# A shallower pipeline over slices in the projection and routing stage, and GpSimd's scatters ahead of later powers

## The reference, cut to what matters

```
x = x + 0.5 * ffn(layernorm(x))
x = x + attn(layernorm(x))
x = x + 0.5 * ffn(layernorm(x))

def ffn(x):
    x = x + msa(layernorm(x, ln1))              # 16 heads of width 8, softmax, projection w_proj
    xf = layernorm(x, ln2)
    expert = argmax(xf @ gate_w + gate_b)       # 8 experts, one per token
    return x + gelu(xf @ w1[expert]) @ w2[expert]
```

## Time and profile before

| | us |
|---|---|
| median of three runs | 1501.73 (1501.5 to 1503.06) |
| the profiled execution | 1514.03 |
| its span in the trace | 1512.0 |
| first projection stage, DVE's first instruction | 427.48 |
| first copy of the expert stage behind it | 509.48 |
| second projection stage, DVE's first instruction | 1319.35 |

### The profile page before, as it was taken

How to read it: one execution, slowest core, us unless ns; L and a number is a source line. 1 busy time by engine, 2 the same in 40 slices (tenths; PEclk the granted TensorE clock), 3 DMA queues, 4 the chain that set the end, 5 groups by cost and what they waited for, 6 DMA issues and landing times. The chain is left out here.

```text
span 1512.0 us, 39416 instructions
## 1 busy us (share of the span) xinstructions
PE 1236.6 (82%) x12592; PEld 694.6 (46%) x12593; DVE 1070.4 (71%) x1896; ACT 856.2 (57%) x1710; POOL 645.7 (43%) x741
## 2 busy tenths in 40 slices
PE   5599999999966497388888747699999999783793
PEld 3234333343356496144455434243333333383793
DVE  8689999999454232478888757899999999182232
ACT  3178888888920253443334315288888888620451
POOL 4304432343337264366665632423323433346362
PEclk9789999999985698599899859599999999865897
DMA  5513342222001121100000005221111211001224
GB/s 175 167 33 88 95 111 62 52 59 47 12 1 48 48 67 50 41 2 3 3 3 2 3 1 223 57 59 49 54 50 50 55 45 44 2 13 53 54 67 122
DMA packets 81640, 81.93 MB, mean 54 GB/s; under 512 B 16265, under 2 KB 53868, under 8 KB 81536
## 3 DMA queue, kind: packets, MB, share of 16 engines
q1 hardware_dynamic: 72704, 70.01, 16.9%
q0 software_dynamic: 4608, 8.44, 1.7%
q10 hardware_dynamic: 4224, 2.10, 0.5%
HBM read 50.56 MB, written 29.93 MB: 53 GB/s over the span
## 5 line engine op out<-in xcount | busy, mean ns | idle before, releaser
L834 DVE TENSOR_REDUCE maxima<-ps 128x2 f32<-128x1024 f32 x512 | 624.1, 1226 | 56.6 <-PE ps L661 47.3
L816 ACT ACTIVATE probs<-ps 128x512 f32<-128x512 f32 x1024 | 552.9, 598 | 78.6 <-PE ps L688 53.2
L661 PE MATMUL ps<-k_stack,q_stack 62*128 62x512 f32 x1024 | 390.4, 478 | 35.4 <-DMA k_stack<-k_split 24.6
L688 PE MATMUL ps<-q_stack,k_stack 64*128 64x512 f32 x1024 | 383.5, 460 | 0.1
L699 PE MATMUL ps<-probs,v_stack 128*32 128x256 f32 x4096 | 328.8, 393 | 1.3 <-ACT probs L816 1.2
L661 PEld LDWEIGHTS ps<-k_stack,q_stack 62*128 62x128 f32 x1024 | 158.5, 193 | 237.5 <-DVE maxima L834 122.9
L620 POOL TENSOR_TENSOR inv<-o_rows,minus_one 128x32 f32<-128x32 f32 x32 | 174.2, 5444 | 29.5 <-ACT o_rows L797 29.5
L688 PEld LDWEIGHTS ps<-q_stack,k_stack 64*128 64x128 f32 x1024 | 162.0, 186 | 13.2 <-ACT probs L816 7.5
L612 POOL CAST neg_wide<-maxima 128x16 fp32r<-128x16 f32 x64 | 12.6, 196 | 357.7 <-DVE maxima L834 357.7
L699 PEld LDWEIGHTS ps<-probs,v_stack 128*32 128x32 f32 x4096 | 81.1, 108 | 171.2 <-issue 122.6
L1314 POOL DMA_INDIRECT expert_out<-yt,number x80 | 78.5, 982 | 71.7 <-issue 45.3
(11 more groups left out here) (203 smaller groups left out, 1660.8 us busy)
## 6 DMA issues: line engine op xcount, KB each, us to landing
q_stack<-q_split SPq DMA_DIRECT2D x256, 64.0 KB
k_stack<-k_split SPq DMA_DIRECT2D x512, 32.0 KB
q_split<-q_parts SPq DMA_DIRECT2D x16, 512.0 KB, 2.7
k_split<-k_parts SPq DMA_DIRECT2D x16, 512.0 KB, 3.4
xt<-sorted SPq DMA_DIRECT2D x80, 64.5 KB
w<-in_L_ffn_w SPq DMA_DIRECT2D x16, 256.0 KB, 3.0
rows<-expert_out SPq DMA_DIRECT2D x16, 256.0 KB, 3.4
x_all<-in_L_attn_x SPq DMA_DIRECT2D x8, 256.0 KB, 3.0
```

Source lines behind the costliest of these rows:

```text
L661: mm = t.matmul(psS[:, h, :], qs[g][score_rows(h), h // 2, u * P:(u + 1) * P], ks[g][score_rows(h), h // 2, :], start=True, stop=True)
L688: t.matmul(ring("e", u, n), ks[g][half(h), h // 2, u * P:(u + 1) * P], qs[g][half(h), h // 2, :], start=True, stop=True).then_inc(e_ready, 1)
L816: a.activation(probs[u % 2][:, h, :], ring("e", u, n), ACT.Exp, scale=float(DK) ** -0.5).then_inc(e_read, 1)
L834: v.tensor_reduce(maxima[i][:, :, pair, u:u + 1], psS[:, 2 * pair:2 * pair + 2, :], AX_X, ALU.max, negate=True).then_inc(s_read, 1)
```

## The change

It rewrites the order of the loops; no instruction is added or taken away, and sizes and buffers stay.

- DVE's turn k now holds `add` of slice k, `norm` of k-1, and of slice k-2 everything from `logits` to `whole`. `places` to `whole` of a slice stand at the end of the turn that began with its `logits`, with `norm` of the slice behind it between.
- PE's turn holds `turn_h` k-2, `project` k+1, `turn_y` k+2, `gate` k-2, `rank` k-2. Two `turn_y` and one `project` run ahead of the loop.
- POOL runs `scale` of slices 0 to 2, and from then on `scatter` of j and `scale` of j+3.

```diff
-                for k in range(SL + 5):
-                    if 1 <= k <= SL:
-                        project(k - 1)
-                    if k < SL:
-                        turn_y(k)
-                    if 4 <= k < SL + 4:
-                        gate(k - 4)
-                    if 3 <= k < SL + 3:
-                        turn_h(k - 3)
-                    if 5 <= k:
-                        rank(k - 5)
+                turn_y(0)
+                turn_y(1)
+                project(0)
+                for k in range(SL + 2):
+                    if k >= 2:
+                        turn_h(k - 2)
+                    if k + 1 < SL:
+                        project(k + 1)
+                    if k + 2 < SL:
+                        turn_y(k + 2)
+                    if k >= 2:
+                        gate(k - 2)
+                        rank(k - 2)
...
-                for k in range(1, SL + 5):
-                    a, n, l, p = k - 1, k - 2, k - 4, k - 5
...
+                for k in range(SL + 2):
+                    adds, norms, picks = k < SL, 1 <= k <= SL, k >= 2
                     if adds:
-                        add(a)
+                        add(k)
+                        moment = moments_of(k)
                     if picks:
-                        pick = logits(l)
+                        pick = logits(k - 2)
...
                     if picks:
                         pick = first(pick)
-                        choose(l, pick)
+                        choose(k - 2, pick)
+                    if norms:
+                        norm(k - 1)
+                    if picks:
+                        whole(k - 2, slots(k - 2, own_places(k - 2, places(k - 2))))
...
-                for k in range(1, SL + 6):
-                    if k <= SL:
-                        scale(k - 1)
-                    if k >= 6:
-                        scatter(k - 6)
+                for j in range(3):
+                    scale(j)
+                for j in range(SL):
+                    scatter(j)
+                    if j + 3 < SL:
+                        scale(j + 3)
```

More of the change, by code:

```diff
@@ L979, in _, with keep_y @@
                 a.activation(rows[:, :, P:], s["token"][:].unsqueeze(2), ACT.Copy).then_inc(numbered, 1)
[L980 to L987, removed]
+                def keep_y(j):
+                    act.wait_ge(y_turned, j + 1)
+                    if j >= 2:
+                        act.wait_ge(projected, j - 1)
+                    a.activation(yT[j % 2][:], psY[j % 2], ACT.Copy).then_inc(y_kept, 1)
+                keep_y(0)
+                keep_y(1)
+                for k in range(SL + 2):
+                    if k >= 2:
+                        j = k - 2
                         act.wait_ge(h_turned, j + 1)
@@ L992, in _ @@
                                      scale=s["ln2_w"][:, 0:1]).then_inc(h_kept, 1)
+                    if k + 2 < SL:
+                        keep_y(k + 2)
             @block.vector
@@ L1101, in whole @@
                     v.tensor_copy(slot[:, tiles_in(j)], slot_f[:]).then_inc(placed, 1)
-                for k in range(1, SL + 5):
-                    a, n, l, p = k - 1, k - 2, k - 4, k - 5
-                    adds, norms, picks, puts = a < SL, 0 <= n < SL, 0 <= l < SL, 0 <= p
+                for k in range(SL + 2):
+                    adds, norms, picks = k < SL, 1 <= k <= SL, k >= 2
                     if adds:
-                        add(a)
+                        add(k)
+                        moment = moments_of(k)
                     if picks:
-                        pick = logits(l)
+                        pick = logits(k - 2)
                     if adds:
-                        moment = moments_of(a)
+                        moment = gather_moments(k, moment)
                     if picks:
                         pick = greatest(pick)
-                    if puts:
-                        put = places(p)
                     if adds:
-                        moment = gather_moments(a, moment)
-                    if puts:
-                        put = own_places(p, put)
+                        variance(k, moment)
                     if picks:
-                        pick = equals(pick)
-                    if puts:
-                        put = slots(p, put)
+                        pick = numbers(equals(pick))
                     if adds:
[L1125 to L1132, removed]
+                        halve(k)
                     if picks:
                         pick = first(pick)
-                        choose(l, pick)
+                        choose(k - 2, pick)
[3 more added lines that the diff above has]
+                        whole(k - 2, slots(k - 2, own_places(k - 2, places(k - 2))))
                 counted = run[SL % 2]
```

## The result

The changed kernel takes 1522.11 us (median of four runs, 1515.42 to 1524.31), the kernel before 1501.62 in the same comparison: ratio 1.0133, interval 1.0095 to 1.0172, 20.5 us slower. The forecast was 1525.0.

A forecast was written before the change was run, and what follows sets the result against it. Bound: the last `places` and the padding behind it. First stage 444.5 + 5 x 8.4 + 2 x 7.3 + 7.7 = 508.8 (+13.4), second +10.1: +23.5 on 1514.03, less 12.3, gives 1525.2 us; range 1486 to 1552.

The forecast's parts named there:

- the head: Start of the first stage up to the first `places`: taken at 444.5, 2.5 us ahead of 446.99.
- the steps: PE-DVE loop per slice: full step 6.3 us at clock 1.00, 9.4 at 0.50; five taken at 8.4.
- The end of the stage hangs on that `places`: Stage end: last `places`, then 10.7 us to the end of the padding; scatters are beside this path.
- last late: Last rank of each stage: its result stays late after the change, adding 7.7 us.
- rival 2: No rank is late in either stage: +8.1 us, 1510 us; chance 0.21.
- The last two: Last two steps of a stage, no projection left: 7.3 us each at clock 0.50, 5.3 at 1.00.
- a third of the time at the upper level: PE's clock over the full steps: mixed, one third at the upper level, giving 8.4 us a step.
- rival 3: Clock stays at 0.50 in both stages: 1536 us, or 1539 with the seventh rank late too; chance 0.18.
- POOL costs and gains nothing: POOL's new order: first scatter at 446 instead of 454.10, no gain since the padding ends later.
- Rival 5: Scatters start and the stage ends 8 us earlier: -16, 1486 us; chance 0.19 together with Rival 1.
- Rival 1: Full clock holds, steps 6.3 and 5.3 us, no late rank: -21.7, 1480 us; chance 0.19 with Rival 5.
- Rivals 3 and 4: Clock 0.50 throughout, 1536 or 1539 us, chance 0.18; every rank late, 1606 us, chance 0.06.

The follow-up runs named there:

- a_again: The changed kernel run once more without an edit: 1525.15 us, ratio 1.0151 to the kernel before.
- b_again: The kernel before run once more without an edit: 1500.23 us, ratio 0.9997.
- b_fill: The kernel before with six unread 128x128 matmuls behind each of PE's turns: 1501.34 us, ratio 0.9998 to the kernel before.
- a_fill2: The changed kernel with six unread matmuls between gate and rank, and more in the last two turns: 1488.43 us, ratio 0.9928 to the kernel before.
- experiment 7: The run b_fill, the kernel before with six unread matmuls behind each PE turn: 1501.34 us, ratio 0.9998.
- experiment 2: The changed kernel with only POOL's old order put back, six powers ahead of the first scatter: 1531.98 us, ratio 1.0206 to the kernel before.
- experiment 3: The kernel before with only POOL's order changed, five powers and then a scatter and a power in turn: 1493.18 us, ratio 0.9948.
- a_reorder: The changed kernel with the projection moved behind the gate in PE's turn: 1517.79 us, ratio 1.0121 to the kernel before.
- experiment 5: The run a_fill2, the changed kernel with unread matmuls up to the last turn: 1488.43 us, ratio 0.9928 to the kernel before.
- a_refill: The kernel of a_fill2 with the projection behind the gate and the further unread matmuls ahead of the gate removed: 1508.54 us, ratio 1.0041 to the kernel before.
- b_padsplit: The kernel before with the padding writes split over the queues of SyncE and ScalarE: 1502.47 us, ratio 1.0019.

## Why the prediction came out, and where it was wrong

The time was within 3 us, but by luck: its errors offset one another. The sum had both stages together 23.5 us longer. Of this, 15.4 us are a late last rank in each stage, which did not come. The baseline's stages were 7.1 us too long, by late ranks of their own, so as much was missing. And the head and the steps were 3 us too short (6 by a_again). That leaves 18.2 us, or 21.2, and 18.2 and 21.1 were measured.

- **What ends the stage: right for after, wrong for before.** "The end of the stage hangs on that `places`" holds in after, by the padding; the last four scatters are at most 1.5 us short of ending it themselves. In before it held only in the profile at hand, where two late ranks pushed the last `places` from about 60 to 67.9 and 71.2 us. In b_again the scatters end 3 us behind the padding, and b_fill shows 10 us of slack on `places`. The baseline stages of the sum were thus 2.5 and 4.6 us too long (82.00 and 84.66 against 79.51 and 80.03).
- **The late ranks: wrong.** The term "last late", +7.7 us in each stage, did not come. The last rank's wait is 2.39 us in after. The condition of rival 2 (no rank late) is what happened. Without that term the working puts the last `places` at 508.8 - 7.7 - 427.48 = 73.6 us from the stage's start; measured 76.2, 74.1 (second stage), 76.8 and 76.5 (a_again). Rival 2's price of 1510 was too low by the baseline: 73.6 and the 14.1 us from the last `places` to the end (90.3 - 76.2) are 87.7, which is 8.2 and 7.7 us longer than b_again's stages, and so some 1516 to 1518 us.
- **The head: nearly.** The first `places` was to come 17.0 us behind the stage's start. It came at 16.7 to 19.0. In three of the four stages of after and a_again part of PE's first chain ran at 0.50: the gate itself in two, the `turn_h` and `project` ahead of it in a third. In the first stage of after the gate is as long as in the earlier trace rows, not the earlier trace rows:

```profile
438.50 1.71 PE L941 MATMUL ps<-gate_w,h2T 128*128 128x8 f32 x8
```

- **The step: right in its prices, lucky in its sum.** A full step at 0.50 was priced at 9.4 us; the row above has 9.41. At 1.00 it was priced at 6.3, and with the clock held it is 5.9 to 6.0. The last two were priced at 7.3 and took 7.4; at the full clock at 5.3, which a_fill2 shows to the tenth. But the sum took five full steps of 8.4 us, 42.0 in all, from a third of the time at the upper level. The five took 42.6, and two misses hide in that. The clock over them was lower, 0.58, about a sixth of the time at the upper level:

```profile
444.57:487.20 42.63, 31.36 (x155) 30.49 (x155) 26.15 (x131) 5.68 (x8) 25.26 (x25) 0.58 0.10 33
```

And only three of the five are full. PE's new order runs `turn_y` and `project` so far ahead that the fourth step (7.4 us) has no `turn_y` left and the fifth (8.1) neither of the two. So three steps have no projection, not two; in the fifth the gate waits for ACT's copy:

```profile
480.85 1.87 PE L941 MATMUL ps<-gate_w,h2T 128*128 128x8 f32 x8 [0.87 <-ACT h2T L997]
```

- **The clock's reason: not supported.** The third of the time at the upper level was worked out from PE's busy share. Neither that value came, as just shown, nor does the share tell the clock: 10.60 busy of 10.60 us stood at 0.50, and 9.93 of 10.60 at 1.00 (experiment 7). The rule of the Trainium skill that was weighed (TensorE: Matmul & The Clock Gate, "HAM oscillation — how this bites in real kernels") puts the loss down to waits between bursts; the page's own case has waits for DMAs, longer than the 2.08 us that PE waits in the step above, so carrying it over to this kernel, as rival 3 did, went beyond the page. After agrees with the rule in part, since two of the three full steps in its first stage took 9.4 us at 0.50; but b_again stood at 0.50 with no wait in PE's rows, so here the measurement decides against taking waits as the only reason.
- **POOL costs and gains nothing: wrong as a general step.** The first scatter stood at 446.37, as worked out. But POOL's order is worth 8 to 11 us within after (experiment 2) and 7.8 us by itself (experiment 3). The prediction let it vanish behind a `places` that was late in that one execution. Rival 5 had the mechanism right and put it in the wrong kernel: combined with short steps it gives the 1488 us of a_fill2, and alone 1493.
- **Rival 1, full clock:** its condition can be had, by unread matmuls; the price of 1480 was too low, since it was counted against the late `places` of the profile at hand. Its last `places` was to stand 486.2 - 427.48 = 58.7 us from the stage's start. In a_fill2 it stands at 58.2, less than 2 us ahead of the 59.7 of b_again; what it gains is the early first scatter (19.6 in place of 29.8).
- **Rivals 3 and 4:** the clock was neither 0.50 throughout nor was any rank late, so neither came. a_reorder, which does stand at 0.50 throughout its window, needs 1517.79 with its shorter steps.

So the cause of the loss was shown by switching it: a step of the three-deep pipeline is a round trip of 7.4 to 9.4 us through PE and DVE, where 5.9 are to be had at granted clock 1.00, and with these the loss is gone (experiment 5). Six deep, the same clock cost the kernel before nothing that its time shows (experiment 7), since POOL's queue ended its stage. Why the clock stays low in one order and not in another is open.

## What to carry to other kernels

A shorter pipeline puts every engine's latency into one loop; price a step of that loop at the clock that the loop itself will get, and look at both levels. Count in which turns every piece of a step is still there: here in three steps of seven. Before a term is taken from a rare row (here waits of 6.7 and 10.0 us beside six plain ones), look whether a second profile of the same kernel has it, since it can also hide which queue ends the stage. Where two branches end a stage, compare when their data landed, not when their rows ended. Split a change that moves two engines: here the half on POOL gains 0.5% by itself and was buried under the other half.

## What the runs showed of the hardware

- Unread matmuls can shorten a kernel: a_fill2 adds over sixty of them to each stage and is 34 us faster than after in the time (1488.43 against 1522.11), with a mean granted clock of 0.97 in the window shown (0.71 and 0.53 in those of after). In a_refill, where they did not hold it, they cost 5.47 us in one turn.
- PE without any gap in its rows was granted 0.50 for 10.6 us (b_again), and 1.00 with less busy time in the same stretch (b_fill, 9.93 us).
- The next stage's first copy came 2.00 and 1.74 us (first and second stage) behind the landing of the padding, on SyncE's queue, where that ended the stage (after, and before as first profiled), and 4.69 and 4.42 us behind the landing of the scatters, on GpSimd's queue, where those did (b_again, b_fill, b_padsplit).
- A rank's result came up to 10 us late in both stages of one profile, with matmul rows of normal length (their ends are modelled) and a closing DRAIN of PE of 9.92 and 10.01 us, and in no profile of thirteen later. Its cause is open; no experiment here could bring it about.
